# One PSUM bank for all side work, issued in bursts, and a third bank for the row maxima

## What is computed

```
x: (2, 2048, 1024); wq, wo: (1024, 1024); wk, wv: (1024, 32)       # 32 query heads of 32, one key/value head
attn(x): q = x@wq; k = x@wk; v = x@wv
         p = softmax(causal(q k^T / sqrt(32)));  return concat_heads(p v) @ wo
ffn(x):  s = 8 * softmax(x@Wr^T + br);  low = x@A^T (8 x 16 columns)
         return 2 * sum over 8 experts of s_h * (low_h @ B_h^T)     # rank 16
x = x + layernorm(attn(layernorm(x)))
x = x + layernorm(ffn(layernorm(x)))
```

## Time and profile before

| | |
|---|---|
| median of 3 runs | 3832.42 us (3829.83 to 3839.87) |
| the profiled execution | 3834.05 us, span of its trace 3832.3 us |
| busy share PE / PEld / DVE / ACT / POOL | 91% / 44% / 65% / 41% / 50% |
| first slot, last slot | 87 us, 3708 us from the span's start |

### The profile page before, as it was taken

The page is one execution under the profiler, slowest core; times in us unless marked ns, Lnnn a source line. Parts: engine busy times, 40 slices in busy tenths (PEclk is TensorE's granted clock), DMA queues, the critical chain, the costliest instruction groups (busy, mean ns, idle before and its releaser), DMA issues.

```text
span 3832.3 us, 47700 instructions
## 1 busy us (share of the span) xinstructions
PE 3486.2 (91%) x17496; PEld 1672.1 (44%) x17496; DVE 2486.3 (65%) x5584; ACT 1584.8 (41%) x3089; POOL 1931.8 (50%) x510
## 2 busy tenths in 40 slices
PE   5799989999999999899998999889999899999984
PEld 3444444444444444444344444444444444444432
DVE  3566786667766666774367677776676756667424
ACT  0233434444444444445433343444444444445541
POOL 0224455545454666656612354565354565667750
PEclk8899999999999999999999999999999999999996
DMA  3312101110110100000121211110100101100000
GB/s 78 118 45 70 45 31 34 56 34 26 32 27 24 52 20 26 25 20 20 56 59 45 70 39 50 34 56 26 39 26 23 32 20 28 32 20 15 18 1 33
DMA packets 132330, 144.19 MB, mean 38 GB/s; under 512 B 28024, under 2 KB 93560, under 8 KB 132096
## 3 DMA queue, kind: packets, MB, share of 16 engines
q1 hardware_dynamic: 132096, 141.13, 12.6%
HBM read 72.91 MB, written 16.78 MB: 23 GB/s over the span
## 4 chain that ended last, share of the span: by engine, by line
PE 70%; DVE 17%; POOL 5%; ACT 3%; issue 2%; SPq 2%; DMA 1%; POOLq 0%; ACTq 0%; DVEq 0%
PE ps L964 13%; PE ps L978 13%; PE ps L993 12%; PE ps L950 10%; PE ps L1100 9%; DVE mx L712 6%; POOL ds L506 4%; DVE ps L729 2%; PE ps L1002 2%; PE ps L1051 2%; PE ps L1142 2%; PE ps L1024 2%; SPq L407 1%; PE ps L967 1%; PE ps L1130 1%
## 5 line engine op out<-in xcount | busy, mean ns | idle before, releaser
L712 DVE TENSOR_REDUCE mx<-ps 128x1 f32<-128x512 f32 (+3 forms) x2560 | 1492.0, 602 | 943.6 <-PE ps L967 473.8
L547 ACT ACTIVATE pr<-ps 128x512 f32<-128x512 f32 (+3 forms) x2560 | 1320.3, 534 | 1603.1 <-PE ps L981 834.7
L506 POOL TENSOR_TENSOR ds<-ds,pr 128x2048 f32<-128x2048 f32 (+3 forms) x384 | 1570.6, 4090 | 494.7 <-ACT pr L547 469.3
L978 PE MATMUL ps<-qs,ks 98*128 98x512 f32 (+3 forms) x2560 | 1354.7, 533 | 46.0 <-ACT pr L547 33.2
L964 PE MATMUL ps<-ks,qs 96*128 96x512 f32 (+3 forms) x2560 | 1043.4, 414 | 168.3 <-DVE mx L712 135.6
L978 PEld LDWEIGHTS ps<-qs,ks 98*128 98x128 f32 x2560 | 492.6, 193 | 747.5 <-ACT pr L547 443.7
L503 POOL TENSOR_TENSOR ds<-pr 128x2048 f32<-128x2048 f32 (+1 forms) x64 | 273.4, 4272 | 957.3 <-ACT pr L547 957.3
L964 PEld LDWEIGHTS ps<-ks,qs 96*128 96x128 f32 x2560 | 503.3, 198 | 351.5 <-DVE mx L712 247.8
L993 PE MATMUL ps<-pr,vs 128*32 128x512 f32 (+3 forms) x5120 | 615.4, 553 | 0.0
L950 PE MATMUL ps<-xT,wq_sb 128*128 128x512 f32 x1024 | 547.7, 619 | 13.9 <-DVE ks L778 12.5
L1100 PE MATMUL ps<-wo_sb,ao 128*128 128x512 f32 x928 | 486.8, 608 | 2.6 <-DVE zs L755 1.4
(11 more groups left out here) (123 smaller groups left out, 2015.7 us busy)
## 6 DMA issues: line engine op xcount, KB each, us to landing
qs<-q SPq DMA_DIRECT2D x768, 64.0 KB, 2.0
wq_sb<-in_L_attn_wq_dram SPq DMA_DIRECT2D x64, 512.0 KB, 3.9
t<-in_L_attn_x_dram SPq DMA_DIRECT2D x32, 512.0 KB, 6.8
xr<-in_L_attn_x_dram SPq DMA_DIRECT2D x32, 512.0 KB, 3.5
out_dram<-xr SPq DMA_DIRECT2D x32, 512.0 KB, 2.7
qs<-mT SPq DMA_DIRECT2D x256, 4.0 KB
wo_sb<-in_L_attn_wo_dram SPq DMA_DIRECT2D x1, 4096.0 KB, 13.7
zs<-in_L_ffn_A_dram SPq DMA_DIRECT2D x1, 512.0 KB
```

Of the source, the lines that this page charges most:

```text
L506: nc.gpsimd.tensor_tensor(ds[:, :, c0:], ds[:, :, c0:], this, ALU.add).then_inc(added, 1)
L547: nc.scalar.activation(pr[:, k % NS, g, c0:], ps[:, PST + g % 2, c0:], ACT.Exp, scale=SCALE).then_inc(exp_done, 1)
L712: nc.vector.tensor_reduce(mx[:, qt * GH + g, c_:c_ + 1], ps[:, PM + g % 2, 0:w], AX.X, ALU.max).then_inc(mx_done, 1)
L978: last = nc.tensor.matmul(ps[:, bank, c0:], ks[0:STK + 2, c:c + P], qs[0:STK + 2, n % NS, g, c0:], start=True, stop=not diagonal)
```

## The change

The output projection, both halves of the transposes, the early part and the weight transposes move into the bank of the q projection, keys and lora (PX = 6). `shared_bank` lists the order of all its users as PE issues them, and `bank_left` waits for the eviction of the user before. Only the first block's transposes, ahead of the slots, take eight banks in turn. The bank that is free is a third one for the maxima (NPM = 3): matmul k of the maxima waits for maximum k-3. The scores still have two banks.

The positions change too. A projection's eight matmuls lie 1.5 positions apart in place of 4 (for q in the first block 3.5, in its u = 5 two); q still begins at 32 (44 in u = 5 where N = 16), the output projection's halves at 64i+48 and 64i+82 (before 64i+32 and 64i+64). Lora's steps are closer together: two transposes at +0 and +3, low at +6, the softmax's second part at +8, slt at +10, the products at +12 and +14 (before +1, +5, +9, +13, +16, +20, +24), and the last tile's lora is in u = 5 in place of u = 6. The norms of the token tiles are at 12, 20, 28 and 36 of u = 4, their transposes at 48 to 62 of u = 4 with evictions in turn by ACT and DVE, the key/value matmuls at 17 to 27 of u = 5. The residual step of `att` is two positions later, at 44. SP stacks q at 63 (before 60), stores at +34 (before +44) and loads the residual at 40 (before 48).

```diff
-        for m, first in ((2, 0), (3, 32)) if n == 0 else ((n + 3, 32),):
+        for m, first in ((2, 0), (3, 32)) if n == 0 else ((n + 3, 44 if u == 5 and N == 16 else 32),):
             if m < UN:
+                apart = 3 if blk or u == 4 else 4 if u == 5 else 7
                 for k in range(KT):
-                    at(64 * u + first + 4 * k, "PE", "q", m, k)
-                for who in ("ACT", "DVE", "SP"):
-                    at(64 * u + first + 4 * (KT - 1), who, "q", m)
+                    at(64 * u + first + apart * k // 2, "PE", "q", m, k)
+                for who in ("ACT", "DVE"):
+                    at(64 * u + first + apart * 7 // 2 + 1, who, "q", m)
+                at(64 * u + (first + 25 if m == n + 2 else 63), "SP", "q", m)
...
-            j, t0 = blk * TB + i, 64 * i + 32
-            at(t0 + 16, "SP", "residual", j)
-            for h in range(2):
+            j = blk * TB + i
+            at(64 * i + 40, "SP", "residual", j)
+            for h, t0 in ((0, 64 * i + 48), (1, 64 * i + 82)):
                 for k in range(KT):
-                    at(t0 + 32 * h + 4 * k, "PE", "proj", j, h, k)
-                at(t0 + 32 * h + 28, "ACT", "proj", j, h)
-            at(t0 + 34, "DVE", "att", j, 0)
-            for k in range(1, 14):
-                at(t0 + 62 + 2 * k, "DVE", "att", j, k)
-            lora(at, t0 + 96 if i < TB - 1 else 64 * 6, j)
+                    at(t0 + 3 * k // 2, "PE", "proj", j, h, k)
+                at(t0 + 11, "ACT", "proj", j, h)
+                at(t0 + 14, "DVE", "att", j, h)
+            for k in range(2, 14):
+                at(64 * i + 96 + 2 * k, "DVE", "att", j, k)
+            lora(at, 64 * i + 128, j)
...
-            at(64 * 4 + 24 + 8 * i, "DVE", "norm", blk, i)
-            for h in range(2):
-                at(64 * 5 + 4 * i + 2 * h, "PE", "tr", blk, i, h)
-            at(64 * 5 + 4 * i, "ACT", "tr", blk, i)
-            at(64 * 5 + 4 * i + 2, "DVE", "tr", blk, i)
+            at(64 * 4 + 12 + 8 * i, "DVE", "norm", blk, i)
+            for h, who in enumerate(("ACT", "DVE")):
+                at(64 * 4 + 48 + 4 * i + 2 * h, "PE", "tr", blk, i, h)
+                at(64 * 4 + 48 + 4 * i + 2 * h, who, "tr", blk, i)
         for k in range(KT):
-            at(64 * 5 + 16 + 2 * k, "PE", "kv", blk, k)
+            at(64 * 5 + 17 + 3 * k // 2, "PE", "kv", blk, k)
...
-        PM, PST, PPV, PQ, PO, PAUX = 0, 2, 4, 5, 6, 7
+        NPM, NPS = 3, 2
+        PM, PST, PPV, PX, PAUX = 0, 3, 5, 6, 7
...
+                        if stage == "tr":
+                            order.append(("tr", 2 * (a[0] * TB + a[1]) + a[2]))
+                        elif stage in ("proj", "early") and a[2] == 0:
+                            order.append((stage, 2 * a[0] + a[1]))
+                        elif stage == "wt":
+                            order.append(("wt", a[0]))
...
                 elif before == "tr":
-                    pe.wait_ge(xt_act, y + 1)
+                    pe.wait_ge((xt_act, xt_dve)[y % 2], y // 2 + 1)
                 elif before == "lora":
                     pe.wait_ge(y2_sb, 2 * (y + 1))
+                elif before == "proj":
+                    pe.wait_ge(z1_ready, y + 1)
...
-                if k >= 2:
-                    pe.wait_ge(mx_done, k - 1)
-                bank, c = PM + g % 2, key_slot(n, c) * BLK
+                if k >= NPM:
+                    pe.wait_ge(mx_done, k - NPM + 1)
+                bank, c = PM + k % NPM, key_slot(n, c) * BLK
```

More of the change, by code:

```diff
@@ L152, in post @@
         for i in range(TB):
[L153 to L155 removed]
+            j = blk * TB + i
+            at(64 * i + 40, "SP", "residual", j)
+            for h, t0 in ((0, 64 * i + 48), (1, 64 * i + 82)):
                 for k in range(KT):
[L157 to L162 removed]
+                    at(t0 + 3 * k // 2, "PE", "proj", j, h, k)
[4 more added lines that the diff above has]
+            lora(at, 64 * i + 128, j)
     def lora(at, t0, j):
         for h in range(2):
[L167 to L174, removed]
+            at(t0 + 3 * h, "PE", "turn", j, h)
+            at(t0 + 3 * h, "ACT", "turn", j, h)
+        for who, *part in (("PE",), ("ACT",), ("DVE", 0)):
+            at(t0 + 6, who, "low", j, *part)
+        at(t0 + 8, "DVE", "low", j, 1)
+        at(t0 + 10, "PE", "slt", j)
+        at(t0 + 10, "ACT", "slt", j)
         for h in range(2):
             for who in ("PE", "ACT", "DVE"):
[L177 removed]
+                at(t0 + 12 + 2 * h, who, "up", j, h)
         for c in range(4):
[L179 to L182, removed]
+            at(t0 + 16 + 2 * c, "DVE", "up", j, 2 + c)
+        at(t0 + 26, "ACT", "out", j)
+        at(t0 + 28, "POOL", "out", j)
+        at(t0 + 34, "SP", "store", j)
     def enter(at, blk):
@@ L347, in bass_mqa_sandwich_lora_router, with shared_bank @@
         SM = 5
-        def projections_bank():
-            order = [("tr", i) for i in range(TB)] + [("kv", 0), ("q", 0), ("q", 1)]
+        def shared_bank():
+            order = [("kv", 0), ("q", 0), ("q", 1)]
             for n in range(UN):
@@ L932, in bank_left @@
             def bank_left(kind, x):
-                before, y = PQ_BEFORE[kind, x]
+                before, y = BEFORE[kind, x]
                 if before == "q":
@@ L949, in project @@
                     bank_left("q", n)
-                last = nc.tensor.matmul(ps[:, PQ, :], wq_sb[:, n % NW, k, :], xT[:, k, :], start=(k == 0), stop=(k == KT - 1))
+                last = nc.tensor.matmul(ps[:, PX, :], wq_sb[:, n % NW, k, :], xT[:, k, :], start=(k == 0), stop=(k == KT - 1))
                 if k == KT - 1:
@@ L1050, in key_values @@
                     pe.wait_ge(xt_dve, TB * (blk + 1))
-                last = nc.tensor.matmul(ps[:, PQ, :], wkv_sb[:, k, :], xT[:, k, :], start=(k == 0), stop=(k == KT - 1))
+                last = nc.tensor.matmul(ps[:, PX, :], wkv_sb[:, k, :], xT[:, k, :], start=(k == 0), stop=(k == KT - 1))
                 if k == KT - 1:
@@ L1129, in lora_low @@
                 for k in range(KT):
-                    last = nc.tensor.matmul(ps[:, PQ, 0:HR + NF], hT[:, k, :], fa_sb[:, k, :], start=(k == 0), stop=(k == KT - 1))
+                    last = nc.tensor.matmul(ps[:, PX, 0:HR + NF], hT[:, k, :], fa_sb[:, k, :], start=(k == 0), stop=(k == KT - 1))
                 last.then_inc(low_ready, 1)
```

120 lines of the change are left out of this document (56 added, 64 removed).

## The result

The changed kernel takes 3814.41 us (median of 15 runs, 3805.32 to 3826.04) against 3834.53 for the kernel before (15 runs): a ratio of 0.9947, 95% interval [0.9935, 0.9959], so about 20 us less where 98 were forecast.

The account below looks back on a forecast made before the run. The prediction took DVE's lag in the maxima as the largest single thing that stops PE. Its terms, -100 - 22 + 8 + 6 + 10 = -98, took 3834 us to 3736, range 3665 to 3820.

Parts of the forecast that it names:

- (f): Projection matmuls gathered in bursts, against the scores' two-bank ring that ACT empties: 0 us, within 40 either way.
- (c): Bare stretch from position 42 to 48: PE waits for DVE's maximum behind the residual step, +8 us, bounds 0 and +90.
- (b): Token tiles' norms at positions 12 to 36 of u = 4: -22 us, bounds -45 and +15.
- (d): Lora's closer steps with nothing beside them: +14 us at N = 16, -8 at N = 64, sum +6.
- (e): One shared bank for all side work, PE waiting for evictions at some changes: +10 us, bounds 0 and +160.
- (a): Third bank for the maxima shortens PE's waits for DVE: -100 us, bounds -60 and -170.
- The rows said to watch: PE's idle time before the maximum matmuls for DVE: from 135.6 to below 60 us, with fewer waits over 2 us.
- the second rival: DVE's lag grows in bare stretches: 3858 us, deciding from 2.4 us per tile; chance 0.12.
- the hand-over rival: Every change of the shared bank costs PE its eviction: 3886 us, shown by over 30 us more waits; chance 0.07.
- (g): SP's new order of stacking q, storing and loading the residual: nothing waits for them, 0 us.
- the wait that moves on: Once DVE no longer stops PE, ACT's exponentials or POOL's adds do: 3802 us; chance 0.21.

Follow-up runs that it names:

- the fixes: Changed kernel with the residual step at position 52, POOL's additions in halves and lora's softmax scaling folded into the next operation: ratio 0.9744 to the kernel before.
- the filling run: Changed kernel with two maxima banks, each maximum matmul in a bare slot issued once more into the empty bank: ratio 1.0514 to the kernel before.

## Why the prediction was wrong

Set against the runs, its sum reads: bursts and the bare stretch they leave (f, c) +8 forecast, +134 measured; norms and lora (b, d) -16, -22; one bank (e) +10, +34; third bank (a) -100, -166. That is -98 against -20. Each figure is one step on one way from the kernel before to the kernel after, and the third bank's shows that another order would give other sizes: 166 us, and 121 with the fixes in.

(f) is the step that failed. It priced the bursts by ACT's ring alone, at 0 within 40, and q's bursts alone, with the residual's step where it was, already cost 42 us. Two things were missing. One is the clock. I charged it only for long waits; the runs show 63 us more lost to it with q in bursts, where the N = 32 unit above stood at 1.2 GHz for 20 us after a wait of 0.93. The other is DVE's lag. DVE catches up with the maxima in slots that carry a side matmul; I had said so of the earlier trace rows, and then gathered these slots without charging the bare ones left behind, except in (c). PE's wait for the maxima shows it for the output projection and the residual (136.0 to 182.3 us), not for q (135.6 to 136.0). What exactly makes the granted clock fall and stay low there is open: PE's modelled busy time (20.41 of 20.50 us) doesn't show it, and the filling run moved the clock the right way without settling it.

(a) was right in kind and direction, and too small: 166 where 100 was taken, near its bound of 170. I took PE's idle rows as the measure (they account for 78 us) and left out the clock (43) and the rest, which may be the weight loads' waits. The worth also depends on the rest, 121 us once DVE's worst lags are gone. The rows said to watch came nearly as forecast: 60.7 us where the line was drawn at 60, and fewer waits over 2 us.

(b) was not tried alone. Its sign (u = 4 at N = 64 below 92 us at a clock above 0.95) failed: 96.4 at 0.91, with the transposes in it. (b) and (d) together came out at -22 for -16, but that is partly luck, as (d) shows: their parts were not where the forecast had them. In the traces the step from bursts alone to all new positions took 34 us off the blocks with N = 32 and 48 and nothing off those with N = 64, and cost 11 in block 4.

(c) was 8 forecast; moving the residual out of the bare stretch is worth 39, cover and fewer held steps together. I priced L818 by its median of before, 1.84 us. It is held about as often as before (over 1.4 us in 19 of 32 tiles, 18 before), but longer just where nothing covers it: in the eight tiles with N = 64 its mean is 3.6 us, 2.5 before, and up to 4.2. The wait of 3.2 us that I computed for the worst case is the 3.17 of the timeline. At 39 / 28 = 1.4 us per tile the second rival's price of 2.4 was not reached by this step alone, but its mechanism was there, and the bursts with it cost 134 / 28 = 4.8.

(d) was right at N = 16: 3.5 us a tile forecast, 14 in all, and block 4 took 11 us more when lora, norms and transposes moved closer (u = 2 of the whole change, 46.4 - 41.4 = 5.0). It was wrong in sign at N = 64. There the softmax's second part met a POOL addition in any case, and earlier it meets one nearer to its start: 2.60 us where it was 1.7. PE's wait for it is 8 x 2.57 = 21 us, of which at most some 0.7 a tile are new, where the forecast took 1 off. The Trainium skill has the rule that I had cited for the long steps ("SBUF — State Buffer", Who interferes with whom: the shared pair is held for the whole instruction). It names no size, and I did not apply it to eight columns; the trace agrees with it, by the 2.60 us.

(e) came out at 34 against 10, within its bounds. PE's waits at L1126, L1144, L1049 and L964 for ACT and DVE rose by 27 us together, under the 30 set for the hand-over rival.

(g) SP's order: PE's wait at the maxima for stacked q is 21.5 us after, 28.2 before. Nothing was lost.

Of the rivals, the wait that moves on to ACT did not come: 38.6 us for 33.2. The time fell near its 3802, and so inside the range of 3665 to 3820 that had been widened for it, for other reasons; that is luck. By the forecast's own line, wrong above 3790, it was wrong.

## What to carry to other kernels

A side matmul between the steps of a ring is cover for the ring's slower consumer. Before gathering such work, charge the steps it leaves bare, at the consumer's duration, and expect that the clock may take more than the waits show, as it did here. A long operation on the engine that shares a port is worth cutting in two where short operations of the other engine sit on the critical path; here halves paid and quarters did not.

Where several edits of one change have large costs of both signs, the sum tells little of any: here 166 us gained and 168 lost made 20 with 22 from the rest.

## What the hardware showed that I had not expected

A DVE operation on 8 columns took up to 2.8 us in the kernel before and 2.60 after, 0.23 at its shortest, because a POOL addition was in progress; cutting the additions in halves took 54 us off a kernel of 3814. The granted clock stood at 1.2 GHz for 20.5 us, with PE busy for 20.41 of them by the profile, after a wait of 0.93 us, while a unit with ten waits up to 1.1 us kept 2.4 GHz. And with two banks for the maxima some 34 to 49 us came that neither PE's idle time nor the clock accounts for, beside 144 us more of waits of the weight loads.
